# Output tiles of an attention slot moved behind all its scores and pieces, with VectorE's additions at the slot's end

## The reference, cut to what matters

```
w_q, w_k, w_v = (codes - 8) * scales            # one scale per 128 rows and column
q, k, v = LN(x) @ w_q, LN(x) @ w_k, LN(x) @ w_v # split into heads, RoPE on q and k
p = softmax(q @ k.T / sqrt(128) + causal mask)  # per head, 512 x 512
a = concat over heads(p @ v) @ w_o
x = x + LN(a)
x = x + LN(down(silu(gate(LN(x))) * up(LN(x))))
```

## Time and profile before

| what | value |
|---|---|
| median of three runs | 1576.78 us |
| profiled execution, its own time | 1574.17 us |
| its span | 1572.4 us |
| PE busy | 1443.0 us (92%) |
| DVE busy | 1294.1 us (82%) |
| ACT busy | 926.2 us (59%) |
| POOL busy | 935.1 us (59%) |
| matmuls | 11104 |

### The profile page before, as it was taken

One profiled execution on the slowest core, in us unless ns is written; L12 is line 12 of the kernel. 1 busy time (PEld: TensorE's weight loads), 2 busy tenths in 40 slices (PEclk: granted clock), 3 DMA queues, 4 the chain that ended last, 5 costly groups with the idle time before them and its releaser, 6 DMA issues.

```text
span 1572.4 us, 40997 instructions
## 1 busy us (share of the span) xinstructions
PE 1443.0 (92%) x11104; PEld 852.1 (54%) x11104; DVE 1294.1 (82%) x2884; ACT 926.2 (59%) x2198; POOL 935.1 (59%) x642
## 2 busy tenths in 40 slices
PE   4778899999999999999999999999999976999998
PEld 2445555556655555555565555556555553544543
DVE  7866689998889898889988999899889885776744
ACT  2465566667667666666667666666666762322421
POOL 2566677777777776777777777777777752110100
PEclk8989899999999999999999999999999987999999
DMA  8379988889889889988888888888988774010000
GB/s 265 61 165 178 166 154 158 158 157 165 158 156 162 155 160 155 167 154 161 158 171 162 163 161 155 161 160 161 166 158 156 142 130 91 14 54 29 26 28 27
DMA packets 522616, 217.15 MB, mean 138 GB/s; under 512 B 478944, under 2 KB 480704, under 8 KB 522432
## 3 DMA queue, kind: packets, MB, share of 16 engines
q1 hardware_dynamic: 519968, 210.53, 70.0%
q0 software_dynamic: 2464, 4.23, 1.5%
HBM read 55.32 MB, written 4.19 MB: 38 GB/s over the span
## 4 chain that ended last, share of the span: by engine, by line
PE 41%; issue 15%; DVE 11%; SPq 11%; DMA 10%; POOL 6%; ACT 4%; DVEq 2%; POOLq 0%; ACTq 0%
DMA ot<-o_parts 6%; DVE prob L1127 4%; SPq L384 4%; PE ps_s L1023 4%; PE ps_s L1024 4%; POOL p_lo L504 4%; PE ps_p L812 3%; PE ps_p L813 3%; PE ps_p L788 3%; PE ps_p L790 3%; PE ps_p L789 3%; DMA swap<-other 2%; PE ps_p L1037 2%; PE ps_p L1038 2%; DVE y L1114 2%
## 5 line engine op out<-in xcount | busy, mean ns | idle before, releaser
L504 POOL TENSOR_TENSOR p_lo<-prob,p_hi 128x1280 f16<-128x1280 f32 x128 | 340.7, 2661 | 175.8 <-ACT p_hi L633 155.5
L1114 DVE SCALAR_TENSOR_TENSOR y<-ps_p,wo_scale,y 128x512 f32<-128x512 f32 x512 | 380.8, 745 | 53.3 <-PE ps_p L813 31.6
L624 ACT ACTIVATE prob<-prob,exp_bias 128x512 f32<-128x512 f32 (+3 forms) x512 | 283.1, 553 | 164.7 <-DVE exp_bias L1136 164.3
L812 PE MATMUL ps_p<-ot,wo 128*128 128x512 f16 x512 | 199.5, 390 | 74.6 <-DMA ot<-o_parts 59.8
L788 PE MATMUL ps_p<-x_hi,w_hi 128*128 128x512 f16 x640 | 245.3, 383 | 5.5 <-DVE w_lo L1048 3.4
L789 PE MATMUL ps_p<-x_lo,w_hi 128*128 128x512 f16 x640 | 244.9, 383 | 0.0
L790 PE MATMUL ps_p<-x_hi,w_lo 128*128 128x512 f16 x640 | 244.7, 382 | 0.0
L1127 DVE CUSTOM_DVE_ANT_0 prob<-ps_s,mask 128x512 f32<-128x512 f32 (+3 forms) x512 | 237.0, 481 | 8.4 <-PE ps_s L827 7.3
L841 PE MATMUL ps_o<-v_hi,ffn_w 128*128 128x128 f16 x1280 | 222.6, 220 | 11.6 <-DVE rot L1102 11.0
L488 POOL TENSOR_TENSOR rot<-rot,swap 128x512 f32<-128x512 f32 x160 | 202.4, 1273 | 46.1 <-DMA swap<-other 45.8
L842 PE MATMUL ps_o<-v_lo,ffn_w 128*128 128x128 f16 x1280 | 222.4, 220 | 0.0
(11 more groups left out here) (100 smaller groups left out, 2979.7 us busy)
## 6 DMA issues: line engine op xcount, KB each, us to landing
swap<-other SPq DMA_DIRECT2D x320, 128.0 KB, 3.0
w_code<-w_codes SPq DMA_DIRECT2D x36, 384.0 KB, 3.7
w_scale<-w_scales SPq DMA_DIRECT2D x36, 384.0 KB, 4.9
o_code<-o_codes SPq DMA_DIRECT2D x35, 256.0 KB, 3.1
swap<-x SPq DMA_DIRECT2D x16, 256.0 KB, 2.8
out<-z SPq DMA_DIRECT2D x16, 256.0 KB, 2.0
ffn_w<-x SPq DMA_DIRECT2D x3, 1024.0 KB, 9.8
ffn_w<-p_hi SPq DMA_TRANSPOSE x128, 3.6
```

Of the source, the lines that this page charges most:

```text
L504: pool.tensor_tensor(p_lo[:, :], prob[:, hp, :], p_hi[:, :], ALU.subtract).then_inc(p_lod, 1)
L624: act.activation(prob[:, hp, a:a + w], prob[:, hp, a:a + w], ACT.Exp, bias=exp_bias[:, hp, i:i + 1], scale=-1.0, accum_out=exp_sum[:, hp, ...
L812: pe.matmul(ps_p[:, bank, :], w, flat(ot[:, hp, 0:TT, :]), start=True, stop=False)
L1114: dve.scalar_tensor_tensor(tile, ps_p[:, bank, :], scale, tile, ALU.mult, ALU.add).then_inc(o_add, 1)
```

## The change

A slot's ring sequence becomes pieces, O0, O1, O2, O3. TensorE makes all three groups of scores, the pieces, and then the four output tiles. VectorE makes the three groups of minima and biases without additions between them, the reciprocal, all takes (V among them), and then the four additions; `dequant` and `w_low` stay behind them. In slot 2 V comes ahead of Q2, on TensorE, VectorE and in the semaphores' counts; ScalarE makes V's high half ahead of the exponential of group 2, and GpSimd makes `rope_add` ahead of `o_low`. No instruction of arithmetic is added or removed.

```diff
-FULL = (("K",), ("Q0", "Q1"), ("Q2", "V"), ("Q3",))
+FULL = (("K",), ("Q0", "Q1"), ("V", "Q2"), ("Q3",))
-START = ("K", "Q0", "Q1", "Q2", "V", "Q3")
+START = ("K", "Q0", "Q1", "V", "Q2", "Q3")
...
-    return ("O0", "O1", "O2") + pieces + ("O3",)
+    return pieces + ("O0", "O1", "O2", "O3")
...                                             # GpSimd, unit
                     p_low(n, h % 2)
+                    roped = [x for x in made_before(U, r, h, slots) if x[2] != "V"]
+                    if first and h == 0:
+                        start_rope("Q3")
+                    else:
+                        for V, vpar, piece, bank, taken in roped:
+                            rope_add(V, vpar, piece, taken)
                     if not (first and h < 2):
                         o_low(n - 2)
                     if first and h == 0:
-                        start_rope("Q3")
                         rope_low(0, 0, "Q3")
                     else:
-                        roped = [x for x in made_before(U, r, h, slots) if x[2] != "V"]
-                        for V, vpar, piece, bank, taken in roped:
-                            rope_add(V, vpar, piece, taken)
                         for V, vpar, piece, bank, taken in roped:
                             rope_low(V, vpar, piece)
...                                             # ScalarE, unit
+                    for V, vpar, piece, bank, taken in made(U, r, h, slots):
+                        if piece == "V":
+                            v_high(V, vpar, bank, taken)
                     if more:
                         exps(n + 1, (h + 1) % 2, 2)
                         p_high(n + 1, (h + 1) % 2)
-                    for V, vpar, piece, bank, taken in made(U, r, h, slots):
-                        if piece == "V":
-                            v_high(V, vpar, bank, taken)
...                                             # TensorE, unit
                     if more:
-                        scores(*nxt, 0)
-                    out_tile(n, h, 0)
-                    if more:
-                        scores(*nxt, 1)
-                    out_tile(n, h, 1)
-                    if more:
-                        scores(*nxt, 2)
-                    out_tile(n, h, 2)
+                        for g in range(NG):
+                            scores(*nxt, g)
                     for piece in slots[h]:
...
-                    out_tile(n, h, 3)
+                    for nt in range(KT):
+                        out_tile(n, h, nt)
...                                             # VectorE, unit
                             lows(n + 1, hp, g)
                             bias(n + 1, hp, g)
-                        out_tile(h, g)
                     invert(n, h)
...
-                        if piece != "V":
-                            take(V, vpar, piece, bank, taken)
-                    out_tile(h, 3)
-                    for V, vpar, piece, bank, taken in made(U, r, h, slots):
-                        if piece == "V":
-                            take(V, vpar, piece, bank, taken)
+                        take(V, vpar, piece, bank, taken)
+                    for nt in range(KT):
+                        out_tile(h, nt)
```

More of the change, by code:

```diff
@@ L663, in _ @@
             rope_high(0, 0, "K")
+            v_high(0, 0, START.index("V") % 2, START.index("V") + 1)
             xt_high(2)
@@ L669, in _ @@
             o_centre(0)
-            v_high(0, 0, START.index("V") % 2, START.index("V") + 1)
             rope_high(0, 0, "Q1")
```

## The result

The changed kernel takes 1645.68 us in the median of four runs (1643.58 to 1649.74), the kernel before 1574.93 us beside it. The ratio is 1.0442, with a 95% interval of 1.0393 to 1.0491: **slower by 4.4%, some 71 us**. The forecast was +31 us, 1605 us, with a range that ended at 1630. The direction and the main mechanism were right; the size was not, and one step carries most of the difference.

A forecast was written before the change was run, and what follows sets the result against it. VectorE, held up by GpSimd, was taken to set the pace at 38.2 us a unit; TensorE's 35.8 + 2.6 handshake + 0.84 hold and loop's end + 0.1 gave 39.3, +31 us over 28 units: 1605 us, range 1574 to 1630.

The forecast's parts named there:

- VectorE sets the pace before, holds included: Kernel before: VectorE's work plus GpSimd's holds and other stalls makes 37.9 us of the 38.2 us unit; TensorE's work is 35.8.
- The handshake: From a slot's last piece through its take to O3: 2.16 us against 1.51, so TensorE loses 0.65 us a slot.
- The hold on `w_low`: End of slot 3: GpSimd's p_low holds VectorE's w_low 0.6 to 1.1 us, costing TensorE 0.45 us a unit.
- the other reading: Hold on VectorE stays at its mean, 1.7 us each wherever put: take 1.3 us late, sum 14 us more.
- The loop's end: TensorE's return between iterations: 2.0 us idle, paid once in four units in place of the 0.45 us hold.
- gains outside the loop against losses: Outside the loop: 2 to 5 us lost at the start and 0 to 5 us more in the last unit, set to cancel.
- Slower still: Rival: p_low slips to just ahead of w_low, slot 0's take 1.9 us late; 40.5 us a unit, 1639 us; chance 0.13.
- Even: Rival: w_low meets no p_low and the loop's end stays covered; 38.4 to 38.6 us a unit, 1580 to 1585 us; chance 0.2.
- Faster: Rival: the wait from last piece to O3 is hidden; 1521 us with no stall, 1567 at half; chance 0.15.
- L814 on L1099: Sign: TensorE's longest wait is for the take, about 0.5 us in nearly every slot, some 110 of them.
- L1045 near 1.7 us: Sign: w_low on VectorE takes nearer 1.7 us than 3.3; 3.3 as now would show the forecast wrong.
- V's wait: VectorE's wait before V's take, 1.1 us a unit, was to go since Q2's matmuls cover V's high half.

The follow-up runs named there:

- e10: Kernel before with one line moved: w_low of slot 3 ahead of the fourth addition instead of behind it; 1529.21 us, ratio 0.9712.
- e9: Changed kernel with w_low of slot 3 moved ahead of the four additions; 1629.66 us, ratio 1.0333.
- e5b: Changed kernel with the first multiplication of each take of a K or Q piece made twice; 1710.07 us.
- e3: Changed kernel with output tile O0 ahead of the pieces, on TensorE and VectorE; 1581.38 us, ratio 1.0046.
- e1: Changed kernel with TensorE's loop of 7 iterations written out straight, other engines as they are; 1607.46 us, ratio 1.021.
- e8: Changed kernel with a wait and 12 more matmuls of 512 columns at the end of each TensorE iteration, output the same; 1634.71 us.
- e7: e4 with V behind Q2, its take behind the additions, ScalarE's and GpSimd's order from before, and w_low ahead of the three additions; 1518.64 us, ratio 0.9629.
- e4: e3 with TensorE's loop written out straight as well; 1566.74 us, ratio 0.9936.
- e11: e7 with TensorE's loop of four units an iteration put back; 1549.82 us, ratio 0.9847.
- e2: Kernel before with TensorE's loop written out straight, nothing else; 1577.48 us, ratio 1.0044.

## Why the prediction was right and wrong

**VectorE sets the pace before, holds included**: right. e10 moves one line, which takes 3.3 us a unit off the holds, and gains 46 us, more than any wait of TensorE's in the list would have promised.

**The handshake, 0.65 us a slot**: right, in place and size. The changed kernel shows the predicted chain in its own trace; e9's 38.3 us a unit is the predicted 38.4; e5b adds its dose four times a unit; in e3 the wait on the take is gone and the time falls by 64 us, where 4 x 0.65 x 28 = 73 stood in the sum.

**The hold on `w_low`**: right in kind. It falls from 2612 to 1755 ns as the start moves later into `p_low`, which is what the Trainium skill (SBUF — State Buffer, "Who interferes with whom") makes of an exclusive lock, and not the unchanged 2.6 us of the other reading. The traces agree: `w_lo` ends 0.81 to 0.82 us behind the end of `p_low` in each of the 22 units between 300 and 1200 us. (For that other reading the prediction gave 14 us more; by its own formula it would be 18.) `dequant` at 949 ns is free, as forecast. Its price is shown in part: 0.45 us were forecast in three units of four. In the trace the wait for the take in slot 0 is 0.51 us in the two units behind a return and 1.04 to 1.45 us in the two others, and 0.51 throughout in e9: 0.3 us a unit, or 8 us of the 16 that e9 gains. Where the other 8 lie was not found.

**The loop's end**: this is the step that failed. The prediction had "TensorE leads and pays it once in four units", at "2.0 from the free start", the idle time read off the kernel before. But that was what its cover left over: the 12 matmuls of a piece, none of which waits, stood in front of the last tile, and the instruction packet of the return started 0.3 to 1.4 us ahead of the last matmul. The change puts the take's wait there and four tiles, and the packet starts 1.1 to 1.3 us behind the last matmul. The whole return comes to light, 3.6 to 4.3 us of idle time, and the clock, which had no term in the sum, falls to its lower level for 2.7 to 5.1 us behind it. Priced at (2.0 - 0.45) / 4 x 28 = 11 us, it costs 38 by e1. e8 shows the cause on TensorE's side: matmuls without a wait ahead of the end bring the idle time to 1.0 to 1.6 us and hold the clock.

The account can be closed from starts of units. From unit 3 to unit 31 pass 1067.9 us before, 1094.8 in e1 and 1131.0 after. So the ends cost 36 us, 6.0 each, and the rest of the loop 27 us, or 0.96 a unit, where the forecast without its loop term had 38.95 - 38.2 = 0.75. Unit 3 is reached 2 us later, and from unit 31 to the end of the span pass 306.3 us against 301.7, where I had set gains outside the loop against losses. That is 36 + 27 + 2 + 5 = 70, for 69.4 us between the two spans. The part outside the loop was not tested further.

**The rivals.** "Slower still" gave 1639 us, near the measured time, but by another cause: `p_low` just ahead of `w_low`. It fell, since `w_lo` has 1755 ns, not 3300; that its number lies close to the measured one is luck. "Even" wanted `w_low` clear of `p_low` and the loop's end covered. e9 brings about the first, with units from 38.3 us up where this rival gave 38.4 to 38.6, and still takes 1630 us: it fell with the loop's end. "Faster" needed a hidden handshake; in the changed kernel it was not. e7, which takes the handshake, the hold and the loop's end away by other edits, comes to 1518.6 us; that this is close to the rival's 1521 says nothing for its mechanism.

**What I said would show it**: L814 on L1099 in 88 slots, VectorE idle before 84 takes, L1045 near 1.7 us, L1055 near 1, all came so. (The 88 are nearly all of the slots between 300 and 1200 us, with 0.60 us each.) A mean slot of 9.8 us was forecast; it is 10.1, through the units that cross an end. V's wait did not go: it is 1.8 us a unit, but in slot 2 Q2's matmuls cover it, and TensorE's wait there is 0.64 us in the mean of 24 units where slot 1, also of two pieces, mostly has 0.49, near the 0.1 us of the forecast; only e4, without the handshake, brought it to light.

## What to carry to other kernels

When buffers go round in a ring, ask of each user how much work lies between the producer that must be read and the one that takes its place; here three tiles (1.3 us) stood against a reply of 2.2 us, and one tile moved ahead of the pieces took the wait away. An idle gap read from a trace is what is left over after its cover: before using it as a price, ask what stood in front of it and whether the change takes that away. And an instruction whose shortest and median durations lie far apart is worth moving by half a microsecond before anything is rebuilt: here one line gave 2.9%.

## What the runs showed of the hardware

- A hardware loop's return on TensorE goes with a 16 KB instruction packet that starts 2.8 to 3.6 us before the first matmul behind it and lands 1.7 to 2.0 us before it (eight kernels, 48 returns between 290 and 1200 us). It leaves 3.4 to 4.4 us of idle time where the packet starts behind the last matmul's start (e3, the changed kernel), 1.0 to 1.6 us with 12 waitless matmuls ahead of it (e8), and 1.2 to 2.2 us in the kernel before.
- All six gaps of 3.6 to 4.3 us in the changed kernel are followed by the lower clock (0.50 for 807 to 812 us), five of the six of 3.3 to 3.9 us in e11 (the gap of 3.31 us is, that of 3.48 us is not), three of the six of 1.9 to 2.2 us in e10 (0.51 for 301.5 to 305 us), none of those of 1.2 to 2.2 us in the kernel before. Idle time alone does not tell. In e11 the matmuls of `attend` have 0.22 us at 600.1 to 601.2 us, behind a gap, and 0.31 from 601.3 on, so the first one's length does not tell either.
- Written out straight, the 28 units of TensorE's loop took 1577.5 against 1573.2 us in the kernel before (e2), 0.2 to 0.6% more, with longer holds of VectorE beside it; e1 has units of 38.6 to 39.8 us but for two of 40.5. No cost of straight code shows apart from that.
- A `w_lo` or `w_scale` that overlaps the end of `p_low` ends 0.81 to 0.82 us behind that end, in every kernel here; free ones take 0.94 to 0.96 us. The two-column bias is held too (means of 0.28 to 0.72 us by kernel, 0.17 when free), and then ends 0.03 us behind a GpSimd instruction in the median; the one-column bias never is (0.152 to 0.156 us in every kernel here).
